# Gates between gathers and picks in a two-layer graph network: layer 0 with twelve a block, layer 1 with its gate for the sums on an earlier gather

## What is computed

```python
# layer 0: a weight matrix per edge, worked out from its 16 attributes
ew  = (edge_attr @ W_e + b_e).reshape(E, 16, 16)
msg = einsum('ei,eio->eo', x[src], ew)
x   = layernorm(x + segment_sum(msg, dst) / max(count, 1) + bias)
# layer 1: a matrix per edge type, and a GRU cell
msg = einsum('emh,eh->em', A[edge_type], x[src])
m   = segment_sum(msg, dst)
x   = layernorm(x + gru(m, x))
```

## The kernel before

| gather | 0 | 1 | 2 | 3 | 4 | 5 | 6 | 7 | 8 | 9 | 10 | 11 | 12 | 13 |
|---|---|---|---|---|---|---|---|---|---|---|---|---|---|---|
| layer 0 | p7 | p8 | p9 | | p10 | o0 | o1 | o2 | o3 | sums | | | o5 | o6 |
| layer 1 | p7 | p8 | p9 | | p10 | | o0 | o1 | sums | | o3 | o4 | | o5 |

## Time and profile before

### The profile page before, as it was taken

How to read it: one execution, slowest core, us unless ns; L and a number is a source line. 1 busy time by engine, 2 the same in 40 slices (tenths; PEclk the granted TensorE clock), 3 DMA queues, 4 the chain that set the end, 5 groups by cost and what they waited for, 6 DMA issues and landing times.

```text
span 5831.4 us, 131035 instructions
## 1 busy us (share of the span) xinstructions
PE 5227.1 (90%) x41758; PEld 4693.1 (80%) x41759; DVE 4199.3 (72%) x5387; ACT 3891.8 (67%) x5533; POOL 3412.9 (59%) x3559
## 2 busy tenths in 40 slices
PE   6999999999999999999978888888888888888887
PEld 5888888888888888888767878788877788788887
DVE  7878787778777788777856666666666666666666
ACT  6666676676666666666566666666666666666664
POOL 6555565555555555555555656655655655655554
PEclk9999999999999999999989999999999999998998
DMA  3111111111111111111111111111111111111110
GB/s 66 33 30 31 33 31 31 31 31 33 30 31 33 30 31 33 31 32 31 25 23 23 23 24 23 23 23 22 23 23 23 23 23 22 24 22 23 23 23 14
DMA packets 330970, 161.25 MB, mean 28 GB/s; under 512 B 193244, under 2 KB 330011, under 8 KB 330771
## 3 DMA queue, kind: packets, MB, share of 16 engines
q1 hardware_dynamic: 218224, 130.59, 9.3%
q0 software_dynamic: 112512, 29.03, 6.3%
q10 hardware_dynamic: 160, 0.80, 0.1%
HBM read 157.44 MB, written 2.66 MB: 27 GB/s over the span
## 4 chain that ended last, share of the span: by engine, by line
PE 63%; issue 15%; DVE 12%; another core or an unknown queue 6%; DVEq 4%; ACT 0%; DMA 0%; POOL 0%; SPq 0%; ACTq 0%
PE psN L752 46%; PE psM L789 15%; DVE cand L953 6%; DVEq L997 2%; DVE nodeT L935 2%; DVE z L991 2%; DVE z L959 1%; DVEq L934 1%; DVEq L952 0%; PE psN L893 0%; PE psM L764 0%; DVEq L958 0%; PE psM L773 0%; DVE grp_hot L943 0%
## 5 line engine op out<-in xcount | busy, mean ns | idle before, releaser
L752 PE MATMUL psN<-table_hi,pick 128*128 128x320 f32 (+1 forms) x13670 | 4080.1, 316 | 167.8 <-DVE cand L953 85.3
L752 PE MATMUL psN<-table_lo,pick 128*128 128x320 f32 (+1 forms) x13670 | 3987.4, 308 | 13.7 <-issue 13.7
L752 PEld LDWEIGHTS psN<-table_hi,pick 128*128 128x128 f32 x13670 | 2598.8, 190 | 306.4 <-issue 226.1
L578 ACT ACTIVATE pick<-dist 128x640 fp32r<-128x640 bf16 (+1 forms) x2485 | 1790.5, 784 | 1336.8 <-PE psN L752 852.8
L752 PEld LDWEIGHTS psN<-table_lo,pick 128*128 128x128 f32 x13670 | 2599.6, 190 | 21.6 <-issue 21.5
L500 POOL DMA_INDIRECT z<-in_x,idx x1761 | 1704.4, 968 | 1176.9 <-issue 417.4
L500 POOL DMA_INDIRECT z<-h_rows,idx x1755 | 1682.2, 959 | 1168.3 <-issue 403.7
L570 ACT ACTIVATE dist<-src_mod,neg_node 128x640 bf16<-128x640 uint16 (+1 forms) x2485 | 1972.6, 874 | 3.3 <-DMA src_mod<-src_mod_rows 3.3
L953 DVE TENSOR_TENSOR cand<-psN,grp_hot 128x640 f32<-128x640 f32 (+1 forms) x1492 | 1122.1, 765 | 1061.3 <-PE psN L752 482.7
L991 DVE TENSOR_TENSOR z<-psD,z 128x2048 f32<-128x2048 f32 (+1 forms) x750 | 1367.8, 1824 | 55.6 <-issue 31.5
L789 PE MATMUL psM<-z,onehot 128*32 128x273 f32 (+1 forms) x12500 | 904.4, 345 | 371.4 <-issue 327.0
(11 more groups left out here) (108 smaller groups left out, 734.3 us busy)
## 6 DMA issues: line engine op xcount, KB each, us to landing
src_mod<-src_mod_rows SPq DMA_DIRECT2D x249, 192.0 KB
src_mod<-src_mod_rows SPq DMA_DIRECT2D x248, 160.0 KB
z<-in_x,idx POOLq DMA_INDIRECT x1761
z<-h_rows,idx POOLq DMA_INDIRECT x1755
eab<-in_edge_attr SPq DMA_DIRECT2D x125, 200.0 KB
idx<-in_src SPq DMA_DIRECT2D x250, 12.5 KB
dstb<-in_dst SPq DMA_DIRECT2D x250, 14.0 KB
grp<-src_grp SPq DMA_DIRECT2D x249, 5.5 KB
```

The costliest lines, as they stand in the source:

```text
L578: act.activation(pick[j][:, CHUNKS[i], 0:hi - lo], dist[i][:, 0:hi - lo], ACT.Relu, bias=1.0, scale=-1.0).then_inc(l["pick_act"], 1)
L752: mm = pe.matmul(rows[:, :, 0:cells.shape[2]], pick[j][:, c, at:at + P], cells, start=(i == 0 and part == 0), stop=(i == TC - 1 and part = ...
```

## The change

The tables are changed, and nothing else.

```diff
-AFTER_OWN = ([{5: 0, 6: 1, 7: 2, 8: 3, 12: 5, 13: 6}] * 2, [{6: 0, 7: 1, 10: 3, 11: 4, 13: 5}] * 2)
-AFTER_SUMS = (9, 8)
-AFTER_LAST = ([{0: 7, 1: 8, 2: 9, 4: 10}] * 2, [{0: 7, 1: 8, 2: 9, 4: 10}] * 2)
+AFTER_OWN = ([{4: 0, 5: 1, 6: 2, 7: 3, 8: 4, 11: 5, 12: 6}] * 2, [{5: 0, 6: 1, 9: 3, 10: 4, 12: 5}] * 2)
+AFTER_SUMS = (10, 7)
+AFTER_LAST = ([{0: 7, 1: 8, 2: 9, 3: 10}] * 2, [{0: 7, 1: 8, 2: 9, 4: 10}] * 2)
```

## The result

The changed kernel takes **5722.6 us** (median of 4 runs, 5721.4 to 5723.6) against 5802.9 (5797.2 to 5810.0) for the kernel before beside it: a ratio of **0.985, 95% interval 0.983 to 0.987**, 80 us less.

What follows compares the result with a forecast made beforehand. Long runs of gathers were taken to hold TensorE's signals and, at the sums, its work. Terms of -24 us (layer 0) and -18 (layer 1) took the 5798.8 us median to 5757; own range 5700 to 5787, 8 in 10: 5695 to 5885.

Steps and rivals of the forecast that it cites:

- The reading: Both layers: a long run of gathers holds TensorE's signals, and at the sums its work; gates matter by shortening runs.
- Layer 0 ahead of the sums: Four gathers ahead of the sums for five, hole shrinks: -0.2 us a block, -24 us, bounds -95 and +300.
- Layer 0 behind the sums: Four gathers behind the sums for five, VectorE's wait for the result may shrink: 0 in the sum, lower bound -35 us.
- Layer 1: The pair of gathers inside the sums comes 0.15 us sooner: -18 us, bounds -50 and +25.
- The sum: Both layers' terms together: -24 - 18 = -42 us, giving 5757 us for the median.
- Rival one: Layer 0: long run moves over the sums' end, delaying transposes; 0.63 us a block, 77 us, total 5858 us; chance 0.33.
- Rival two: Layer 1 falls to the lower clock more often: 40 more blocks cost 64 us, 5839 us; chance 0.05.
- Rival three: Whole kernel: gates already met, held signals independent of the gathers, so no change, 5799 us; chance 0.15.
- Four gathers in the run ahead: Sign of being right, layer 0: four gathers, not five, in the run ahead of the sums.
- The mean below 22.89: Sign of being right, layer 0: mean time per block below 22.89 us.
- The hole below 0.78: Sign of being right, layer 0: TensorE's hole inside the sums shorter than 0.78 us.
- VectorE's wait at or under 1.53: Sign of being right, layer 0: VectorE's wait before adding the result at or under 1.53 us.

Runs made afterwards that it cites:

- first chip: Chip of the change's first measurement: changed kernel 5722.6 us against 5802.9 for the kernel before; whether it is one of the four follow-up chips is not on record.
- A: Follow-up chip with late signals, used for one layer or one part at a time; the kernel before took 5794.7 us.
- C: Follow-up chip with late signals; kernel before 5812.4 us, changed kernel 5732.1 us (0.985), kernel before with four gathers left out 5597.0 us (0.962).
- ahead only: Kernel before with only layer 0's gates ahead of the sums changed (gather 3 for pick 10, 4 to 8 for own picks 0 to 4): 5702.4 us, 0.984.
- behind only: Kernel before with only layer 0's gates for and behind the sums changed (sums on 10, own picks 5, 6 on 11, 12): ratio 1.001.
- B: Follow-up chip without late signals; kernel before 4915.8 us with four gathers left out, 4916.0 without gates, changed kernel 4915.6, all ratio 1.000.
- D: Follow-up chip without late signals; kernel before 4915.6 us; the changed kernel and the version with layer 0's new gates only took 4916.0 and 4916.1, ratio 1.000.
- layer 0 alone: Kernel before with all of layer 0's new gates and layer 1's old ones: 5678.3 us, ratio 0.980, where signals were late.

## Why the prediction came out as it did

**The reading** (a long run of gathers holds TensorE's signals, and its work at the sums) holds on the first chip, A and C: one gather less in the run ahead shortened the sums by 0.61 us (ahead only), a run behind the sums that is broken by two gates took VectorE's wait away (behind only), and four fewer took 1.77 us off the block. It lacks a condition that the trace of before couldn't show: on B and D the same runs of gathers hold nothing, and the kernel takes 4916 us whatever its gates. It also underrated the matter: I counted TensorE's busy time as work, but between the same marks the sums' 50 multiplications take 426.0/125 = 3.41 us a block on B and 540.0/125 = 4.32 in the earlier trace rows. The holes that I priced (117 us) are about half of what the late sums cost (1.86 us a block, 227 us). And one reading was off: own pick 0's last multiplication starts at 1443.90 and ends at 1444.21; the row at 1444.19 belongs to the next pick. So gather 5 was 4.05 us late and not 3.76. The record of the signal stands at 1448.00.

**Layer 0 ahead of the sums: right in sign, far too small.** I took -0.2 us a block, -24 us, and gave -95 as the lower bound. The part alone measured -92 us on chip A. The mechanism was right; the term that was mis-sized is this one, and the step behind it is the choice between the ends: the block at 1518.44, 2.47 us slower, pulled the value towards nothing, and the lower end held no more than the hole. The part's gain lay at two places, 0.61 us in the sums and 0.31 before the next sums, less 0.17 before pick 0.

**Layer 0 behind the sums: 0 in sum was right alone, and wrong in company.** Alone it is nothing (ratio 1.001, medians 5794.3 and 5794.7), but it is a sum of effects that cancel: VectorE's wait goes, as I thought possible, and what followed from it was larger than my bound of 0.29: 0.21 us at pick 0 and 0.29 before the next sums, 0.50 in sum, since the bound was read from one block and not from the mean. The other effect I had not seen: without its gate gather 9 joins 5 to 8 in one run of five over the sums, which with the more frequent falls of the clock costs 0.51 us. The 0 came out by luck. With the shorter run ahead the part gains: layer 0 alone is 24 us below ahead only. But in the whole change VectorE's wait, which I expected to shrink, stays (204.0 to 194.9 us), since the late signal of the sums makes gathers 10 to 13 a run of four over the result, and only TensorE's wait behind it goes (the group of the first halves of picks loses the 29.5 us that had ended with a selection).

**Layer 1: the size was right, the path to it only in part.** I took -18. About -16 is left when layer 0's 64 are taken from 80. The blocks of layer 1 at the full clock say the same without that difference: 22.11 us after for 22.30 before on the first chip, 22.12 for 22.28 on C (the run with four gathers of layer 0 left out has the old gates in layer 1), 0.18 and 0.15 a block before rounding, for the forecast 0.15. Alone, on chip A, it gave -35. But the shift from which I worked it out, 0.15 us sooner, was there only in part: over the layer the pair's first gather starts 0.52 us into the sums before and 0.47 after on the first chip (medians), 0.54 and 0.43 on C, 0.57 to 0.66 and 0.29 on A. So that the number fits is partly luck. One block of layer 1 in the changed kernel, its sums on TensorE, then gathers 5 and 7:

```profile
4154.63 1.32 PE L789 MATMUL psM<-z,onehot 128*32 128x128 f32 x33 [0.62 <-DVE z L991]
```

```profile
4154.93 0.95 POOL L500 DMA_INDIRECT z<-h_rows,idx  x1 [1.36 <-PE psN L752]
...
4158.75 0.95 POOL L500 DMA_INDIRECT z<-h_rows,idx  x1 [1.62 <-PE psM L789]
```

The pair starts 0.30 us into the sums, for 0.70 in the earlier trace rows, as the signs asked; the block of the earlier trace rows was later than the median of its own layer.

**The sum.** -24 and -18 were forecast; about -64 and -16 came. The miss, 38 us in the difference (34 in the time itself, as the kernel before took 4 us more beside the changed one), is layer 0's. It lies within the stated range of 5700 to 5787.

**Rival one** did happen, at about two thirds of its price and not as a net loss: 0.40 us a block before the transposes, for 0.63. Its mechanism is the one named: signalled late (1.39 us), copied late by ScalarE, waited for by TensorE (28 us of idle time at the transposes, and 0.40 x 122 = 49 us in all). Its point of decision was wrong. It needs no run longer than three at the sums' end; the pair 8 and 9 is enough when it is still on. And the gain ahead, which I left out of its sum, was larger than it.

**Rival two** did not come; layer 1 had fewer blocks at the lower clock, 8 for 25. The Trainium skill (TensorE: Matmul & The Clock Gate, "HAM oscillation — how this bites in real kernels") says that kernels whose matmuls pause in each round keep falling back; by that rule a stretch of such blocks could come or go as a whole. The traces agree: with the same old gates in layer 1, one profile has 25 such blocks and four others have 8, 12, 8 and 15. In each of these traces falls stand 20 blocks apart; in the one of before three of them last 7, 6 and 8 blocks, in the one of after none lasts more than one. Why every twentieth block is open. **Rival three** (no change) is what B and D show, though for another reason: there the gates do bind, and TensorE never waits for what they delay (on B 579.9 us of GpSimd's idle time ended with a pick).

**The signs.** Four gathers in the run ahead: seen. The mean below 22.89: 22.36. The hole below 0.78: not in the block shown (1.04), but the group's idle time fell from 117.1 to 105.9. VectorE's wait at or under 1.53: not in the block shown (2.06), though the group's fell from 204.0 to 194.9; there VectorE is done sooner and the signal comes no sooner after gather 13 (1.27 us, for 1.46).

**What stays open.** What makes a chip one with late signals. Whether the whole change or layer 0 alone is faster: the same gates of layer 0 gave 22.34 and 22.36 us a block in the whole change (first chip, C) and 21.99 alone (A). Old gates of layer 0 took 22.88 on the first chip and 22.96 on A, so a quicker chip is no explanation by itself; and a gate of layer 1 cannot act on layer 0, which runs before it, through any wait. Layer 0's and layer 1's parts on A would add up to 151 us, the whole gave 80. The kernel without any gate was measured only where signals are not late, so what all the gates together are worth where they are late is not known.

## What to carry to other kernels

Where a trace shows signals of one engine late behind runs of another's indirect DMAs, first look whether another chip shows them too: here that is worth 15% of the time (5800 against 4916 us), and no edit tried gained more than 4%. Then place the runs so that none is on when a signal is raised that others wait for: here the ends of the sums and of the result are such places. A gate that binds also breaks a run: the same four gathers held the result's signal when they went as one run over its end, and did not when two gates made them pause. And price a stage by its length between marks against the same stage undisturbed, since the engine's busy time hides a part of the loss.

## What was not expected of the hardware

One and the same kernel takes 5795 to 5812 us on two chips (and 5803 on the first) and 4916 us on two others, and steadily so: 33 runs of the kernel before on B lie within 4914 and 4920 us. TensorE's granted clock hardly differs (0.979 to 0.990 for 0.996 or 0.997). GpSimd's gathers take the same 0.95 us on either kind of chip, 0.30 us apart. What differs is when a signal of TensorE comes: on B it is recorded within 0.02 us of its pick's end, on the others most come 0.8 to 1.5 us after a gather has ended.

The two kinds of chip differ in one more thing in the trace. The kernel before left 41512 records of semaphore updates on the first chip; the changed kernel left 97222 on B and 97239 on D, and between 40551 and 43235 in every profile of the full work with late signals, although all raise the same semaphores. Most of what is missing are updates by DMAs (30346 for 80422). So on a chip with late signals "remote" or "issue" behind an idle time says little about what ended it, and the starts and ends of the instructions have to carry the argument, as they do here.
